# Decoder layer with routed experts: the adds of the shared expert's result, the second slot's gathered rows and the last slot's order are rearranged

## The reference, cut

```python
x = x + attention(layernorm(x))                         # linear attention, 16 heads
x = x + long_convolution(ctx, ctx, layernorm(x))        # Toeplitz products with context
h = layernorm(x).reshape(2048, 512)
w, sel = route(h)                                       # 16 experts, top 4 of 2 groups
out = sum over experts e of cw[:, e] * (silu(h @ g[e].T) * (h @ u[e].T)) @ d[e].T
shared = (silu(h @ sg.T) * (h @ su.T)) @ sd.T           # one shared expert, all tokens
return x + out + shared
```

## Time and profile before

| what | us |
|---|---|
| median of the 3 timed runs | 900.91 (899.61 to 901.28) |
| the profiled execution | 908.35 |
| its span, first to last instruction | 906.1 |
| TensorE busy | 864.7 |
| VectorE, ScalarE, GpSimd busy | 571.2, 376.8, 377.3 |
| mean granted clock of TensorE | 0.983 of full |

### The profile page before, as it was taken

How to read it: one execution, slowest core, us unless ns; L and a number is a source line. 1 busy time by engine, 2 the same in 40 slices (tenths; PEclk the granted TensorE clock), 3 DMA queues, 4 the chain that set the end, 5 groups by cost and what they waited for, 6 DMA issues and landing times.

```text
span 906.1 us, 14066 instructions
## 1 busy us (share of the span) xinstructions
PE 864.7 (95%) x4380; PEld 710.9 (78%) x4380; DVE 571.2 (63%) x890; ACT 376.8 (42%) x608; POOL 377.3 (42%) x385
## 2 busy tenths in 40 slices
PE   8899999999989999999999999799999999999994
PEld 7788888888867777777887777577787777777784
DVE  5766766656569999999769856254354543544431
ACT  5312322233034433443552345355564555645552
POOL 1200000001036686551522324566665666656644
PEclk9999999999989999999999999899999999999998
DMA  8500000000026533330211377878888888898856
GB/s 294 184 1 1 0 0 0 0 0 13 1 69 198 167 113 105 117 106 18 94 48 23 125 257 190 173 189 194 198 183 207 198 195 196 185 200 204 193 107 88
DMA packets 50963, 109.45 MB, mean 121 GB/s; under 512 B 8881, under 2 KB 11441, under 8 KB 50801
## 3 DMA queue, kind: packets, MB, share of 16 engines
q0 software_dynamic: 17024, 40.48, 23.8%
q1 hardware_dynamic: 33904, 68.55, 23.7%
HBM read 78.35 MB, written 30.65 MB: 120 GB/s over the span
## 4 chain that ended last, share of the span: by engine, by line
PE 62%; DVE 18%; issue 10%; DMA 4%; ACT 3%; POOL 1%; POOLq 0%; DVEq 0%; SPq 0%; ACTq 0%
PE PS L198 16%; PE PS L200 16%; PE PS L199 16%; PE PS L209 6%; DVE QY L965 5%; PE PS L1530 2%; PE PS L638 2%; PE PS L567 2%; DVE term L959 2%; DVE term L949 1%; DVE QY_rounded L1781 1%; ACT hTh L1325 1%; DMA X<-in_x 1%; DMA out_y<-QY,idy 1%; DVE wl L1776 1%
## 5 line engine op out<-in xcount | busy, mean ns | idle before, releaser
L198 PE MATMUL PS<-QY_rounded,wh 128*128 128x512 f32 (+1 forms) x376 | 154.1, 410 | 1.7 <-DVE QY_rounded L1781 0.9
L200 PE MATMUL PS<-QY_rounded,wl 128*128 128x512 f32 (+1 forms) x376 | 146.9, 391 | 0.0
L1254 POOL DMA_INDIRECT out_y<-QY,idy x72 | 118.1, 1640 | 42.8 <-ACT QY L1344 26.6
L199 PE MATMUL PS<-QY_rounded,wh 128*128 128x512 f32 (+1 forms) x312 | 120.3, 386 | 0.0
L1794 DVE TENSOR_TENSOR hTl<-hh,hTh 128x512 fp32r<-128x512 f32 (+1 forms) x39 | 26.5, 678 | 125.3 <-ACT hTh L1325 121.1
L1236 POOL DMA_INDIRECT xg<-xs_d,idx x72 | 84.9, 1180 | 32.3 <-issue 15.8
L209 PE MATMUL PS<-qER,Tz 128*128 128x288 f32 x320 | 82.6, 412 | 4.5 <-DVE low_rounded L805 2.4
L268 POOL TENSOR_SCALAR var_eps<-mean_var 128x2 f32<-128x2 f32 x14 | 4.9, 351 | 191.8 <-DVE mean_var L394 191.8
L200 PEld LDWEIGHTS PS<-QY_rounded,wl 128*128 128x128 f32 x376 | 71.0, 189 | 15.2
L198 PEld LDWEIGHTS PS<-QY_rounded,wh 128*128 128x128 f32 x376 | 71.7, 191 | 13.6 <-issue 1.1
L209 PE MATMUL PS<-prod,Tz 128*128 128x288 f32 x320 | 82.2, 412 | 0.1
(11 more groups left out here) (221 smaller groups left out, 1854.1 us busy)
## 6 DMA issues: line engine op xcount, KB each, us to landing
ws<-in_gu_w SPq DMA_DIRECT2D x38, 512.0 KB
ws<-in_dn_w SPq DMA_DIRECT2D x20, 512.0 KB, 5.6
C<-in_ctx SPq DMA_DIRECT2D x32, 256.0 KB, 2.6
Tz<-kpad_d SPq DMA_DIRECT2D x32, 256.0 KB, 3.2
xs_d<-xn SPq DMA_DIRECT2D x16, 256.0 KB, 2.0
out_y<-X SPq DMA_DIRECT2D x16, 256.0 KB
X<-in_x SPq DMA_DIRECT2D x1, 3072.0 KB, 16.0
xg<-xs_d,idx POOLq DMA_INDIRECT x72
```

Of the source, the lines that this page charges most:

```text
L198: pe.matmul(out_, lh, rh, start=first, stop=False)
L199: pe.matmul(out_, lh, rl, start=False, stop=False)
L200: return pe.matmul(out_, ll, rh, start=False, stop=last)
L1254: nc.gpsimd.indirect_dma_start(out=out, out_offset=bass.IndirectOffsetOnAxis(ap=idy[:, t:t + 1], axis=0), in_=yo[:, t], in_offset=None, co ...
```

## The change

- Shared group 3: tiles 2 and 3 of its down projection and their ACT copies move from slot 0's gate-up to the transposes of slot 0. On DVE the sums of group 0 move behind the last shared hidden values, those of group 1 behind `x_lo(0, 3)`, and those of group 3 from slot 1 to before slot 0. SP's stores of group 3 move ahead of part 2 of slot 1's weights.
- Second slot: its gathered rows go into buffers of their own (`second`, over the memory of `prod[0]` and `xn3_all`, which is free by then), with semaphores of their own. `gathers(1)` follows `gathers(0)` at once, `gathers(2)` waits for slot 0 alone, and slots 0 to 2 take their indices without a copy.
- Last slot: PE does three of the four blocks d of the first half, then the `down5` of the slot before, then the fourth block; ACT's silu of that half moves behind the four `y_out`.

```diff
@@ -1044,6 +1044,8 @@
         xg = sb("xg", [P, SLOT_T, D + NE])
+        second = [flat[:, 0:2 * (D + NE)].rearrange("p (t n) -> p t n", t=2) for flat in
+                  (prod[0][:].rearrange("p c b n -> p (c b n)"), xn3_all[:].rearrange("p k n -> p (k n)"))]
         idx = sb("idx", [P, SLOT_T], U32)
@@ -1115,11 +1117,23 @@
         xg_in = [sem(f"xg{t}_in") for t in range(SLOT_T)]
+        second_in = [sem(f"second{t}_in") for t in range(SLOT_T)]
         xT_ps5, xT_hi5, xT_lo5 = sem("xT_ps5"), sem("xT_hi5"), sem("xT_lo5")
...
         iota_done, tri_done, val_hot = sem("iota_done"), sem("tri_done"), sem("val_hot")
+
+        def is_second(s):
+            return isinstance(s, int) and s == 1
+
+        def rows_of(s, t):
+            return second[t // 2][:, t % 2] if is_second(s) else xg[:, t]
+
+        def rows_in(s, t):
+            if is_second(s):
+                return second_in[t], 16
+            return xg_in[t], 16 if isinstance(s, int) and s == 0 else 16 * s
 
@@ -1204,14 +1218,12 @@
                 next_part(e, 0, 1)
-                for g in range(NG - 1):
+                for g in range(NG):
                     store_group(g)
...
                 e = expert_of(sp, 2)
-                next_part(e, 1, 0)
-                next_part(e, 1, 1)
-                store_group(NG - 1)
-                next_part(e, 1, 2)
+                for part in range(NPART):
+                    next_part(e, 1, part)
                 middle_slots(sp, next_slot, more)
@@ -1226,23 +1238,31 @@
 
-                def gathers(s, first=False):
-                    if not first:
-                        wait_apart(pool, xT_ps5, DC * s)
-                        wait_apart(pool, wpos_done, s)
+                def gathers(s):
+                    fixed = isinstance(s, int) and s < 3
+                    if not fixed or s == 2:
+                        wait_apart(pool, xT_ps5, DC if fixed else DC * s)
+                        wait_apart(pool, wpos_done, 1 if fixed else s)
+                    if not fixed:
                         nc.gpsimd.tensor_copy(idx[:], IDX[:, bass.ds(SLOT_T * s, SLOT_T)]).then_inc(idx_done, 1)
-                        wait_apart(pool, idx_done, s)
+                        wait_apart(pool, idx_done, s - 2)
                     for t in range(SLOT_T):
-                        nc.gpsimd.indirect_dma_start(out=xg[:, t], out_offset=None, in_=xs_d,
-                                                     in_offset=bass.IndirectOffsetOnAxis(ap=(IDX if first else idx)[:, t:t + 1], axis=0)
-                                                     ).then_inc(xg_in[t], 16)
+                        at_ = IDX[:, SLOT_T * s + t:SLOT_T * s + t + 1] if fixed else idx[:, t:t + 1]
+                        nc.gpsimd.indirect_dma_start(out=rows_of(s, t), out_offset=None, in_=xs_d,
+                                                     in_offset=bass.IndirectOffsetOnAxis(ap=at_, axis=0)
+                                                     ).then_inc(rows_in(s, t)[0], 16)
 
...
                     for t in range(SLOT_T):
-                        wait_apart(pool, xg_in[t], 16 * (s + 1))
+                        wait_apart(pool, *rows_in(s, t))
                     e = expert_of(pool, s)
-                    nc.gpsimd.tensor_copy(WPOS[:, bass.ds(SLOT_T * s, SLOT_T)].unsqueeze(2), xg[:, :, bass.ds(e + D, 1)]
-                                          ).then_inc(wpos_done, 1)
+                    if is_second(s):
+                        nc.gpsimd.tensor_copy(WPOS[:, SLOT_T:SLOT_T + 2].unsqueeze(2), second[0][:, :, bass.ds(e + D, 1)])
+                        nc.gpsimd.tensor_copy(WPOS[:, SLOT_T + 2:2 * SLOT_T].unsqueeze(2), second[1][:, :, bass.ds(e + D, 1)]
+                                              ).then_inc(wpos_done, 1)
+                    else:
+                        nc.gpsimd.tensor_copy(WPOS[:, bass.ds(SLOT_T * s, SLOT_T)].unsqueeze(2), xg[:, :, bass.ds(e + D, 1)]
+                                              ).then_inc(wpos_done, 1)
 
@@ -1294,13 +1314,13 @@
                 wait_apart(pool, idx_ready, 1)
-                gathers(0, first=True)
+                gathers(0)
+                gathers(1)
                 more = more_slots(pool)
...
                 weights(0)
-                gathers(1)
+                gathers(2)
                 weights(1)
-                gathers(2)
                 wait_apart(pool, x3_out, 16 * NT)
@@ -1345,9 +1365,6 @@
                 def next_parts(s, final=False):
-                    if isinstance(s, int) and s == 0:
-                        y_shared_out(NG - 1, 2)
-                        y_shared_out(NG - 1, 3)
                     hid_hi(s + NG, 0)
@@ -1360,9 +1377,12 @@
                     w_hi(s, 1)
-                    silu(s + NG, 0)
+                    if not final:
+                        silu(s + NG, 0)
                     for t in range(SLOT_T):
                         y_out(s - 1, t, second)
+                    if final:
+                        silu(s + NG, 0)
                     next_parts(s, final)
@@ -1420,7 +1440,9 @@
                 x_hi(0, 2)
+                y_shared_out(3, 2)
                 x_hi(0, 3)
+                y_shared_out(3, 3)
                 act.wait_ge(es_done, 2)
@@ -1526,8 +1548,8 @@
                         if d == 0:
-                            pe.wait_ge(xg_in[t], 16 * (s + 1))
-                        mm = pe.transpose(PS[:, 4 + d % 2, t * P:(t + 1) * P], xg[:, t, d * P:(d + 1) * P], ident[:])
+                            pe.wait_ge(*rows_in(s, t))
+                        mm = pe.transpose(PS[:, 4 + d % 2, t * P:(t + 1) * P], rows_of(s, t)[:, d * P:(d + 1) * P], ident[:])
                     mm.then_inc(xT_ps5, 1)
@@ -1540,12 +1562,15 @@
                     first = isinstance(s, int) and s == 0
-                    for d in range(DC):
+                    ahead = 3 if final else DC
+                    for d in range(ahead):
                         slot_gate_up(s, 0, d)
...
                             down5(s - 1 + NG, t)
+                    for d in range(ahead, DC):
+                        slot_gate_up(s, 0, d)
                     if final:
@@ -1557,9 +1582,6 @@
                             slot_gate_up(s, 1, d)
-                            if first and d == 0:
-                                down5(NG - 1, 2)
-                                down5(NG - 1, 3)
                             x_transposed(s + 1, d)
@@ -1610,8 +1632,8 @@
                     x_transposed(0, d)
-                    if d == 1:
-                        down5(3, 1)
+                    if d > 0:
+                        down5(3, d)
                 pe.wait_ge(es_done, 2)
@@ -1804,8 +1826,6 @@
                     w_lo(s, 1)
-                    if isinstance(s, int) and s == 1:
-                        add_shared(NG - 1)
                     hidden(s, 0)
@@ -1817,14 +1837,15 @@
                 w_lo(0, 0)
-                add_shared(0)
                 hidden(-1, 1)
                 hid_lo(-1, 1)
-                add_shared(1)
+                add_shared(0)
                 w_lo(0, 1)
...
                     x_lo(0, d)
+                add_shared(1)
                 add_shared(2)
+                add_shared(3)
                 dve.wait_ge(es_done, 2)
```

## The result

| | before | after |
|---|---|---|
| median, us | 901.1 (899.61 to 901.62, 4 executions) | 895.83 (895.63 to 898.4, 4) |
| profiled execution, its span | 908.35, 906.1 | 898.4, 896.1 |

The ratio is 0.9942 by the medians and 0.9939 [0.9915, 0.9963] by pairs: 5.3 us faster, where 8.7 were forecast, and half a microsecond above the range. The two profiled executions differ by 10.0 us of span. Both numbers are right, and the difference between them is the subject of this study.

A forecast was written before the change was run, and what follows sets the result against it. TensorE was busy 95% of the span, its longest idle a 5.3 us y_out wait in slot 2. Terms 0.3 + 0.2 + 7.9 + 0.9 - 0.1 = 9.2, taken as 8.7: 900.91 - 8.7 = 892.2 us, range 890.6 to 895.3 (about 85%).

The forecast's parts named there:

- Slot 2's period becomes 18.9: gain 26.80 - 18.9 = 7.9: Slot 2: earlier stores of X remove TensorE's wait for y_out and the half clock behind it; 7.9 us.
- discounted by 0.5 us: Whole sum: profiled execution 7.4 us over the median, so half a microsecond off the stall's transfer times; 8.7 for the median.
- Rival B: Slot 2's stall: timed runs stall less than the profile, landing times shorter without profiler; gain 4 to 6, 895 to 897; 0.13.
- Shared sums and slot 0: Slot 0: small waits melt into one of about 2.3 us for x_lo, hidden(0,0) 1.1 late; gain 0.3 us.
- rival A: Slot 0: clock falls after the new 2.3 us wait, costing 1.3; gain 7.4, 6.1 at worst, 893.5 to 894.8; 0.28.
- Own buffers: Slots 0 and 1: earlier gathers end the waits for rows, slot 1's period falls from 19.12 to 18.9; gain 0.2 us.
- Stores ahead: Slots 0 to 2: stores of X land at 543, scatters(0) start 0.8 behind y_out, slot 2's wait goes; 7.9 us.
- The last slot: Last slot: final scatters no longer wait for scatters(16), first one 0.8 behind its y_out; gain 0.9, cost 0.1.
- C: Slot 2: scatters(0) may not wait for the stores, so only the end gains 0.9; 900.0 us; chance 0.05.
- D: Slot 0, DVE: block of twelve sums ends late and delays slot 1; 899.6 at twice the sum time; chance 0.04.

The follow-up runs named there:

- sums_behind: The kernel after with shared group 3's four sums moved from ahead of hidden(0,0) to behind x_lo(1,1): 894.37 us, ratio 0.991 [0.988, 0.994] to the kernel before.
- buffers_only: The kernel before with only the second slot's own buffers and the gathers' new order: 899.2 us, ratio 0.9971 [0.9955, 0.9986].
- no_buffers: The kernel after without the second slot's own buffers and early gathers: 899.85 us, ratio 0.9964 [0.9943, 0.9985] to the kernel before.
- late_group3: The kernel after with group 3's sums and stores back where they were: 895.96 us, ratio 0.9942 [0.9923, 0.9962] to the kernel before.
- end_only: The kernel before with only the last slot's new order: 901.48 us, ratio 0.9993 [0.9972, 1.0014].

## Why the prediction was off

**The step that failed** is "Slot 2's period becomes 18.9: gain 26.80 - 18.9 = 7.9". The mechanism was read rightly and the change does remove it; the period after is 18.90. But 26.80 isn't what the median execution pays. All three traces at 905.1 or more have that stall and neither of the two below has it; 19 of 110 executions are that long, and the profile happened to be one. The usual one loses 2.1 to 2.2 us in slots 1 and 2 together, mostly to gathered rows, and the kernel after gives 1.6 of it back when its clock falls. Stage for stage, the means of the two traces of the usual kind before (901.27, 903.98) and of the three after:

| stage | forecast | measured | from |
|---|---|---|---|
| ahead of slot 0 | 0 | 1.9 | first transpose at 519.4 and 520.7, after 517.5 to 519.0; 0.3 is the change's, the rest open |
| slot 0 | 0.3 | 0.9 | 19.48 and 19.78, after 18.69 |
| slots 1 and 2 | 8.1 | 1.2 (0.6 to 2.4) | 39.9 and 40.0; after 39.3, 39.3 and 37.7 |
| end | 0.8 | 1.8 | 320.3 and 321.1 from there on, after 318.8 to 319.1 |
| sum | 9.2, of which 8.7 for the median | 5.8 | 5.3 timed |

For the profiled execution the sum of 9.2 met 10.0 of span, and that is partly luck. Slots 1 and 2 gave 6.6 of the 8.1, because the clock fell; 1.7 came from ahead of slot 0, where nothing was forecast; slot 0 gave 0.5 and the end 1.2.

The warning stood in the prediction's own numbers: an execution 7.4 us above the median of its kernel, with one stall of 5.3 and a half clock that no other slot has. It was discounted by 0.5 us. The better reading was that the excess over the median was about the size of the stall and its half clock (5.3 + 2.6), so the median might not have them. Rival B said so at 0.13.

**Shared sums and slot 0.** Right in form: one wait for x_lo, 2.1 where 2.3 was forecast, and hidden(0,0) 1.1 late behind the twelfth sum. The gain was put at 0.3 and is 0.9 by the table. The wait has a price that the sum left to rival A: `sums_behind` shows that the block costs 1.1 by itself, and the clock now and then 1.6 more.

**Own buffers.** No wait for gathered rows is left in any of the three traces after, as forecast. The size, 0.2, was read from the same unusual trace; usual ones wait 1.8 to 2.0 us for rows in slot 1, and `buffers_only` is worth 0.29% [0.14, 0.45], 2.6 us. It also lets the down projections move. But no part carries the change alone: `no_buffers`, with all the rest, is worth 0.36% [0.15, 0.57].

**Stores ahead.** Scatters(0) 0.9 behind `y_out`, no wait for L1364, full clock at 570: all as forecast, and worth nothing in the median once the other parts are in (`late_group3`). The long executions are gone, 19 of 110 before at 905.1 or more and the 14 after within 4.1 us. That isn't shown to be the stores' doing: of the 24 executions of `late_group3` and `buffers_only`, which have the stores late and the buffers, none is above 900.91. The Trainium skill (DMA: Bandwidth & Descriptors, "Issuing engines are not separate DMA queues") agrees with the traces: transfers of SP and POOL were in each other's way, and the last scatter landed in 8.1 to 9.0 us with SP's load 1.6 us behind it, in 6.01 with the load held.

**The last slot.** The first final scatter starts 0.80 behind its `y_out`, as forecast. The time is shorter by the 0.8 predicted or somewhat more: from the transpose d = 2 of slot 3 to the last scatter's issue it is 311.5 in the three traces after and in `end_only`, and 312.3 to 313.0 in the five before.

**The rivals.** A happened, in two traces of three (20.4 and 20.4 for 18.8 in slot 1), at 1.6 us against 1.3 forecast; the prediction gave it as a case that holds or doesn't, and it is a chance of each execution. The Trainium skill (TensorE: Matmul & The Clock Gate, "HAM oscillation — how this bites in real kernels") lays the fall at longer idle gaps than these 2.1 us; the traces differ, with half clock behind five of nine single waits of 1.8 to 2.2 us. B named the right time, 895 to 897, and the right outcome, that most timed runs stall less than this profile. Its reason isn't needed: profiled executions of 901.27 and 903.98 have no such stall either, and 16 timed ones are as long as those that have it. C and D didn't happen; the twelve sums ran at 0.62 each.

**Open.** Ahead of slot 0, the order of the change is worth 0.3 us that nobody forecast. From the end of the routing's last result (`IDX`) on VectorE to the first transpose it is 10.6 us in the five traces before and in `buffers_only`, and 10.3 in all kernels where group 0's sums stand behind the last shared hidden values. In the former TensorE steps by 0.42 and 0.33 us once, where 0.23 is usual (at 901.27):

```profile
516.11 0.40 PE L200 MATMUL PS<-wh,hTl 128*128 128x512 f32 x1
516.53 0.50 PE L198 MATMUL PS<-wh,hTh 128*128 128x512 f32 x1
516.86 0.39 PE L199 MATMUL PS<-wl,hTh 128*128 128x512 f32 x1
```

The rest of the 1.9 lies ahead of that point, where the programs are the same: over all kernels the first transpose comes from 517.5 to 520.8, and so few traces don't tell chance from effect. Open are also why the rows come late in some executions and not in others, and what the stores ahead would be worth without the rest.

## What to carry to other kernels

Before a stall in a trace is given a price, compare that execution with the timed ones: where it is longer than the median by about the stall, suspect that the stall made it long and that the median doesn't pay it; a few more traces of the same kernel tell. Where two parts of a change both gain, ask whether they remove the same loss. Where a transfer's rival is issued by the progress of the very engine that waits for it, expect two kinds of executions. And look at short waits that recur in every slot before the one big one: sixteen of 0.3 us, from the helper engines doing two tasks in the wrong order, gave more than the whole change.

## What the runs showed of the hardware

- The last of four accumulating scatters of 128 rows landed 8.1 to 9.0 us after its issue with a 512 KB load issued 1.6 us behind it (three traces), and after 5.4 to 5.7 with the load 3.1 us or more behind (three traces of the same order). With the load held until the landing it was 6.01. In two kernels of another order it was 6.5 and 6.8 with the load 3.8 us behind.
- TensorE's clock went to half within 1.4 us behind five of nine single waits of 1.8 to 2.2 us, and stayed whole behind the other four. In the kernel after that was twice in three traces (0.79 and 0.80 over five microseconds, 1.00 in the third), at 1.6 us each. Behind waits of 1.0 us in slot 0 it stayed whole in both traces that have them alone (`late_group3`, `sums_behind`); behind 4.4 to 5.3 us it fell in all three.
- A wait of TensorE that the profile gives as 0.29 cost 0.45 from start to start (0.69 for 0.24) and 0.52 of the period, because the matmul ahead of it is drawn 0.40 long while the next one can start after 0.24 (586.03 and 586.27).
